# Value products of the wide attentions, stacked to full rows with 32-row bands in pairs

## The chip, the cores and the metric

One core of one Trainium2 chip. The time is device microseconds of one execution. Engines: PE is TensorE (PEld its weight loads), DVE VectorE, ACT ScalarE, POOL GpSimd, SP the queue that issues DMAs.

## The reference, cut to what matters

x has 128 sequences of 64 tokens with 128 features, the context `ctx_768` 128 sequences of 64 tokens with 96 features. Four layers follow each other, each an attention of x to the context and a feed-forward part, both added to x. The attentions that the change touches are L0 (8 heads of 128) and L2 and L3 (16 heads of 64):

```python
q = (layernorm(x) @ Wq) ; k = context @ Wk ; v = context @ Wv      # split into heads
attn = softmax(q k^T * scale)                                       # within a sequence, 64 x 64
x = x + (attn @ v).reshape(...) @ Wo + bo
```

## The kernel before, in words

`wide_attention` (L408) does one such attention. The product Wv Wo of each head is computed at its start ("fold": `fold_bank`, four heads a round, two rounds in L0, four in L2 and L3), so a value has 128 features per head: 96 context features times M. fp32 products that must be exact are made of three passes of a faster format (fp32r): high and low part of each operand, high*high, low*high, high*low (`product`, L285; its matmuls are L288, L290, L291). ScalarE keeps the high part of M (`keep_folded`, L690), VectorE the low one (`keep_rest`, L786). The context is loaded by SP in groups of 512 tokens, 96 rows (192 KB), and GpSimd splits it into high and low (`split_context`, L389 and L392), the next group's one while a group is worked on.

The 8192 tokens go in 16 groups of four tiles of 128 tokens. A group has Q steps of four heads, Q = 2 in L0 and 4 in L2 and L3 ("paired": two heads of 64 share 128 rows). That makes 32, 64 and 64 steps. In step m TensorE (`group` under `block.tensor`) does, in an order written out by hand: projections 0 and 1, three passes of 512 columns each; the transposes of the probabilities of step m - 2 (L577); projections 2 and 3; the four value products (`value`, three passes each, one PSUM bank per 128 tokens, each with 96 rows); the outputs of step m - 2 (L598, 64 matmuls in 64x64 tiles); the scores of step m (64 matmuls, in 64x64 tiles at L617, in L0 96x64 at L620). Values of four steps are held (`step % 4`). PSUM banks 4 to 7 rotate: P0, P1, T0, T1, P2, P3, V0 to V3 take them in turn, banks 0 and 1 are the scores', 2 and 3 the outputs'.

Besides, in each step: ScalarE copies projections (L708), transposed probabilities (L718) and values 0 and 2 (L713) out of PSUM and takes exponentials (L723); VectorE makes maxima and their subtraction (L810, L813), totals and inverses (L818, L821) and copies values 1 and 3 (L825), and once per group normalises and splits the next x (L254, L256); GpSimd multiplies probabilities by the inverses (L511). Every engine waits on semaphores that the others count up.

In L1 the narrow attention has scores in 32x64 tiles (L1030), which the change doesn't touch.

## Time and profile before

| | us |
|---|---|
| median of 3 runs (lowest, highest) | 3561.42 (3557.74, 3566.69) |
| the profiled execution | 3553.97 |
| its span, first to last instruction | 3552.1 |

The attentions of L0, L2 and L3 take about 353, 618 and 622 us of the span. A timeline row gives start, length, engine, line, operation, output and inputs, the part of the array (rows*columns of weights), the moving operand's shape and how many instructions are merged in it; a row of several runs from the first's start to the last's end. Matmuls overlap, so the distance of starts is what one costs.

### The profile page before, as it was taken

How to read it: one execution, taken by the hardware profiler on the slowest of the kernel's cores; microseconds unless marked ns; L12 is line 12 of the kernel's file. 1: busy time of each engine (PE TensorE's matmuls, PEld its weight loads, DVE VectorE, ACT ScalarE, POOL GpSimd, SP SyncE). 2: the span in 40 equal slices, each digit the busy share in tenths (PEclk: the TensorE clock that was granted, in tenths of full speed). 3: DMA queues.
4: the chain of work that ended last, by engine and by line, in shares of the span. 5: the costliest groups of instructions: out<-in, count | busy, mean ns of one | idle time of the engine just before them, and what ended most of it. 6: DMA issues, size and time to landing. Idle time of an engine off the chain costs nothing. (4 is left out here: it accounts for less than half of the span.)

```text
span 3552.1 us, 99744 instructions
## 1 busy us (share of the span) xinstructions
PE 3412.4 (96%) x43493; PEld 2808.9 (79%) x43493; DVE 2473.8 (70%) x4946; ACT 2033.0 (57%) x3467; POOL 1244.1 (35%) x923
## 2 busy tenths in 40 slices
PE   7999899999999899999999989999999998999999
PEld 6888788887888555788888878878888886777777
DVE  8977555555667799666666667766666666777776
ACT  4445555554666688455555545555555555566564
POOL 1322133334554233222222223322222224555555
PEclk9999999999999999999999999999999999999999
DMA  3000000001000000000000000010000000000000
GB/s 110 11 11 11 1 1 1 1 1 38 15 15 8 1 1 1 23 9 7 7 9 7 5 22 1 1 47 9 7 7 9 7 5 1 7 7 13 7 7 13
DMA packets 15488, 41.03 MB, mean 12 GB/s; under 512 B 2959, under 2 KB 4687, under 8 KB 14158
## 3 DMA queue, kind: packets, MB, share of 16 engines
q1 hardware_dynamic: 15054, 34.64, 3.2%
q8 instruction: 345, 5.65, 0.7%
q14 instruction: 89, 0.73, 0.1%
HBM read 30.44 MB, written 4.19 MB: 10 GB/s over the span
## 5 line engine op out<-in xcount | busy, mean ns | idle before, releaser
L708 ACT ACTIVATE projL<-bank 128x512 f32<-128x512 f32 (+1 forms) x640 | 371.3, 601 | 646.0 <-PE bank L291 630.4
L511 POOL TENSOR_TENSOR probL<-probL,invL 128x1024 f32<-128x1024 f32 x160 | 304.5, 1903 | 1196.5 <-DVE invL L821 1196.5
L1704 POOL TENSOR_TENSOR h_loM<-hM,h_hiM 126x512 fp32r<-126x512 f32 x224 | 290.3, 1296 | 254.7 <-ACT h_hiM L1830 252.0
L598 PEld LDWEIGHTS bank<-valuesL,probTL 64*64 64x64 f32 x10240 | 277.7, 133 | 60.9 <-issue 55.0
L810 DVE TENSOR_REDUCE neg_maxL<-bank 128x16 f32<-128x1024 f32 x160 | 195.9, 1224 | 183.7 <-PE bank L617 152.9
L598 PE MATMUL bank<-valuesL,probTL 64*64 64x128 f32 x10240 | 316.4, 272 | 4.4 <-ACT probTL L718 4.4
L1403 PEld LDWEIGHTS bank<-w2T,hM 128*128 128x128 f32 x2304 | 276.8, 192 | 39.3 <-ACT hM L1458 24.1
L1403 PE MATMUL bank<-w2T,hM 128*128 128x128 f32 x2304 | 283.4, 276 | 16.2 <-ACT hM L1458 16.2
L1458 ACT ACTIVATE hM<-bank,ahead_scales 128x512 f32<-128x512 f32 x288 | 183.8, 684 | 189.3 <-PE bank L291 189.0
L825 DVE COPY valuesL<-bank 128x512 f32<-128x512 f32 x320 | 213.1, 679 | 107.2 <-PE bank L291 101.3
L818 DVE TENSOR_REDUCE totalL<-probL 128x16 f32<-128x1024 f32 x160 | 194.8, 1217 | 122.4 <-ACT probL L723 122.1
L1381 POOL TENSOR_TENSOR accM<-accM,partM 128x512 f32<-128x512 f32 x128 | 165.0, 1289 | 295.5 <-DVE partM L1488 295.5
L1942 DVE TENSOR_TENSOR tM<-bank,siluM 126x512 f32<-126x512 f32 x224 | 154.2, 689 | 115.2 <-PE bank L291 64.6
L713 ACT ACTIVATE valuesL<-bank 128x512 f32<-128x512 f32 x320 | 195.4, 611 | 54.9 <-PE bank L291 54.2
L1830 ACT ACTIVATE h_hiM<-hM 126x512 fp32r<-126x512 f32 x224 | 140.6, 628 | 132.5 <-DVE hM L1966 131.3
L718 ACT ACTIVATE probTL<-bank 128x512 f32<-128x512 f32 x320 | 188.4, 591 | 24.9 <-PE bank L577 24.8
L813 DVE TENSOR_TENSOR probL<-bank,neg_maxL 128x1024 f32<-128x1024 f32 x160 | 195.9, 1225 | 5.5
L1824 ACT ACTIVATE siluM<-bank 126x512 f32<-126x512 f32 x224 | 132.0, 589 | 97.4 <-PE bank L291 95.7
L1488 DVE TENSOR_TENSOR partM<-bank,gatesM 128x512 f32<-128x512 f32 x128 | 88.4, 691 | 128.3 <-PE bank L1403 127.1
L723 ACT ACTIVATE probL<-probL 128x1024 f32<-128x1024 f32 x160 | 169.4, 1059 | 2.9 <-DVE probL L813 2.8
L577 PEld LDWEIGHTS bank<-ident,probL 128*128 128x128 f32 x1280 | 149.5, 141 | 24.0 <-POOL probL L511 1.8
L577 PE MATMUL bank<-ident,probL 128*128 128x128 f32 x1280 | 166.6, 273 | 0.5 <-POOL probL L511 0.3
(309 smaller groups left out, 9050.0 us busy)
## 6 DMA issues: line engine op xcount, KB each, us to landing
ct0L<-in_ctxP SPq DMA_DIRECT2D x24, 192.0 KB, 2.5
ct1L<-in_ctxP SPq DMA_DIRECT2D x24, 192.0 KB, 2.5
x<-in_x SPq DMA_DIRECT2D x4, 1024.0 KB, 10.9
out<-x SPq DMA_DIRECT2D x8, 512.0 KB, 2.6
nct<-in_ctxP SPq DMA_DIRECT2D x16, 192.0 KB, 2.4
ahead_second<-in_L0w SPq DMA_DIRECT2D x2, 1152.0 KB, 18.1
ahead_second<-in_L3gate SPq DMA_DIRECT2D x1, 882.0 KB
ahead_second<-in_L3up SPq DMA_DIRECT2D x1, 882.0 KB
```

The source lines that it names most:

```text
L511: nc.gpsimd.tensor_tensor(segments(prob[:, slot, :]), segments(prob[:, slot, :]), per_segment(inv[:, slot, :]), ALU.mult).then_inc(prob_re ...
L577: last = nc.tensor.transpose(rot.bank(step, f"T{half}")[:, u * P:(u + 1) * P], prob[:, prob_slot, cols], c.ident[:, :])
L598: last = nc.tensor.matmul(o_bank[b * SEQ:(b + 1) * SEQ, t, u * D:(u + 1) * D], probT[t * SEQ:(t + 1) * SEQ, 2 * s + u, b * SEQ:(b + 1) * SEQ],
L708: nc.scalar.activation(proj[:, u, :], rot.bank(step, f"P{u}")[0:rows, :], ACT.Copy, scale=scale if paired and u % 2 == 0 else 1.0).then_in ...
L713: nc.scalar.activation(values[:, step % 4, u, :, :].rearrange("p h d -> p (h d)"), rot.bank(step, f"V{u}")[:, :], ACT.Copy).then_inc(Veven ...
L718: nc.scalar.activation(probT[:, 4 * half:4 * half + 4, :].rearrange("p s q -> p (s q)"), rot.bank(step, f"T{half}")[:, :], ACT.Copy).then_ ...
L810: nc.vector.tensor_reduce(neg_max[:, prob_slot, :], segments(s_bank.rearrange("p h c -> p (h c)")), axis=AX.X, op=ALU.max, negate=True).th ...
L813: nc.vector.tensor_tensor(segments(prob[:, prob_slot, :]), segments(s_bank.rearrange("p h c -> p (h c)")), per_segment(neg_max[:, prob_slo ...
L818: nc.vector.tensor_reduce(total[:, prob_slot, :], segments(prob[:, prob_slot, :]), axis=AX.X, op=ALU.add).then_inc(total_ready, 1)
L825: nc.vector.tensor_copy(values[:, step % 4, u, :, :].rearrange("p h d -> p (h d)"), rot.bank(step, f"V{u}")[:, :]).then_inc(Vodd_kept, 1)
L1403: last = nc.tensor.matmul(y_bank[ex % NY][:, t * D:(t + 1) * D], h[:, (n + j) % NH, t * P:(t + 1) * P], W2[:, 2 * ex + j, :], start=(t == ...
L1704: nc.gpsimd.tensor_tensor(h_lo[:, a % SLOTS, :], h[:, a % 3, :], h_hi[:, a % SLOTS, :].bitcast(F32), ALU.subtract).then_inc(lo_ready, 1)
```

## The change

The value product of 128 tokens is no longer three passes over 96 rows. Three operands of 128 rows are stacked instead. With H and L the high and low parts and a, b, c the three 32-row bands of the 96 context features:

- T1 holds Ha Hb Hc La, M1 the matching Ha Hb Hc Ha: one full pass;
- T2 holds Ha Hb Lb Lc, M2 the matching La Lb Hb Hc: one full pass;
- T3 holds Hc alone, the band u of it (rows 32u to 32u + 31) that of token tile u, M3 has Lc four times: one pass of 32 rows for each tile, done for tiles 0 and 1 together after the second tile, and for 2 and 3 after the fourth.

SP loads the context three times stacked (A and B with 128 rows, 256 KB each, C 64 KB), GpSimd rounds and subtracts in place (`stack_context`); in paired layers it also keeps `ct_lo` for the projections. The outputs of step m - 2 move ahead of value product 3. Values are held for three steps. The folded rounds are kept by three copies and five differences each, on VectorE; in L2 and L3 rounds 2 and 3 are done in steps 1 and 2, and TensorE waits for each round by itself. The fourth fold bank moves from bank 7 to banks 0 to 3. VectorE splits the next x before it copies value 3.

```diff
@@ wide_attention @@
-        M_hi, M_lo = (sb(f"M{n}{tag}", [K, heads, D], F32R) for n in ("_hi", "_lo"))
+        M1, M2, M3 = (sb(f"M{n}{tag}", [P, heads, D], F32R) for n in (1, 2, 3))
...
-        values = sb(f"values{tag}", [P, 4, 4, 4, D])
+        values = sb(f"values{tag}", [P, 3, 4, 4, D])
...
-        fold_bank = (c.bank[1], c.bank[2], c.bank[3], c.bank[7]) if paired else (c.bank[1], c.bank[3])
+        fold_bank = c.bank[0:4] if paired else (c.bank[1], c.bank[3])
+        parts = 6 if paired else 5
@@ block.sync @@
-                first_contexts(sp, c, "ctxP", ct, ct_in)
+                def load_context(j):
+                    for dst, name in zip(raw[j % 2], ("ctxA", "ctxB", "ctxC")):
+                        cols = dst.shape[1]
+                        sp.dma_start(dst[:, :], dram[name][:, j * cols:(j + 1) * cols]).then_inc(ct_in[j % 2], 16)
+
+                load_context(0)
+                load_context(1)
...
-                later_contexts(sp, c, "ctxP", ct, ct_in, S_done, Q, 0)
+                for j in range(2, NG):
+                    sp.wait_ge(S_done, (j - 1) * Q)
+                    load_context(j)
@@ block.gpsimd @@
+                def stack_context(j, slot):
+                    A, B, C = raw[slot]
+                    pool.wait_ge(ct_in[slot], 48 * (j // 2 + 1))
+
+                    def high_part(part, high):
+                        nc.gpsimd.tensor_tensor(high[:, :], part[:, :], c.one[:, :].to_broadcast([P, part.shape[1]]), ALU.mult)\
+                            .then_inc(ct_split, 1)
+
+                    high_part(A, T1[slot])
+                    if paired:
+                        pool.wait_ge(ct_split, parts * j + 1)
+                        nc.gpsimd.tensor_tensor(ct_lo[slot][:, :], A[0:K, :], T1[slot][0:K, :].bitcast(F32), ALU.subtract)\
+                            .then_inc(ct_split, 1)
+                    high_part(B, T2[slot])
+                    high_part(C, T3[slot])
+                    for n, (part, high, rows) in enumerate(((A, T1[slot], slice(96, P)), (B, T2[slot], slice(64, P)))):
+                        pool.wait_ge(ct_split, parts * (j + 1) - 2 + n)
+                        nc.gpsimd.tensor_tensor(high[rows, :], part[rows, :], high[rows, :].bitcast(F32), ALU.subtract)\
+                            .then_inc(ct_split, 1)
+                    pool.wait_ge(ct_split, parts * (j + 1))
@@ block.tensor @@
-                    pe.wait_ge(lo_kept, 2 * rounds)
+                    pe.wait_ge(lo_kept, rounds)
...
-                    weights = tuple(M[:, 4 * k:4 * k + 4, :].rearrange("p h d -> p (h d)") for M in (M_hi, M_lo))
-                    product(nc, rot.bank(step, f"V{u}")[:, :], (ct_hi[slot][:, tok], ct_lo[slot][:, tok]), weights)\
-                        .then_inc(V_done, 1)
+                    for n, (tokens, weights) in enumerate(((T1, M1), (T2, M2))):
+                        nc.tensor.matmul(rot.bank(step, f"V{u}")[:, :], tokens[slot][:, tok],
+                                         weights[:, heads_of, :].rearrange("p h d -> p (h d)"), start=(n == 0), stop=False,
+                                         skip_group_check=True)
+
+                def values_rest(slot, k, step, pair):
+                    for u in (2 * pair, 2 * pair + 1):
+                        band = slice(32 * u, 32 * u + 32)
+                        nc.tensor.matmul(rot.bank(step, f"V{u}")[:, :], T3[slot][band, :],
+                                         M3[band, 4 * k:4 * k + 4, :].rearrange("p h d -> p (h d)"), start=False, stop=True,
+                                         skip_group_check=True).then_inc(V_done, 1)
...
-                            pe.wait_ge(ct_split, 2 * i + 2)
...
+                        if k == 0 and paired:
+                            pe.wait_ge(ct_split, parts * i + 2)
...
-                        if m == 0 and paired:
-                            pe.wait_ge(lo_kept, 6)
+                        if k == 0:
+                            pe.wait_ge(ct_split, parts * (i + 1))
+                        if i == 0:
+                            pe.wait_ge(stack_kept, k + 1)
                         value(m, slot, k, 0, step)
                         pe.wait_ge(T_kept, 2 * m + 2)
                         value(m, slot, k, 1, step)
+                        values_rest(slot, k, step, 0)
                         pe.wait_ge(P_kept, 4 * m + 7)
                         value(m, slot, k, 2, step)
                         if older:
                             wait_for_output(n, *back)
+                            if paired and i == 0 and k == 2:
+                                pe.wait_ge(stack_kept, 4)
+                            output(n, back[0], back[1], n % 3)
                         wait_for_scores(m, i, k)
                         value(m, slot, k, 3, step)
-                        if older:
-                            output(n, back[0], back[1], bstep % 4)
+                        values_rest(slot, k, step, 1)
+                        if paired and i == 0 and k == 0:
+                            pe.wait_ge(stack_kept, 2)
                         scores(m, i, slot, k)
@@ block.vector @@
+                def stack_copies(r):
+                    dve.wait_ge(hi_kept, r + 3 if paired else 2 * r + 2)
+                    for M, to, rows in ((M1, slice(96, P), slice(0, 32)), (M2, slice(64, 96), slice(32, 64)),
+                                        (M2, slice(96, P), slice(64, 96))):
+                        nc.vector.tensor_copy(flat(M, to, r), fold_bank[r][rows, :])
+
+                def stack_differences(r):
+                    nc.vector.tensor_tensor(flat(M2, slice(0, 64), r), fold_bank[r][0:64, :],
+                                            flat(M1, slice(0, 64), r).bitcast(F32), ALU.subtract)
+                    for u in range(4):
+                        last = nc.vector.tensor_tensor(flat(M3, slice(32 * u, 32 * u + 32), r), fold_bank[r][64:96, :],
+                                                       flat(M1, slice(64, 96), r).bitcast(F32), ALU.subtract)
+                    last.then_inc(stack_kept, 1)
...
-                keep_rest(0)
-                keep_rest(1)
-                if paired:
-                    keep_rest(2)
-                    keep_rest(3)
+                    keep_rest(0)
+                    keep_rest(1)
                     for scale_step in scale_steps:
                         scale_step()
                 else:
+                    keep_low_queries(0)
+                    keep_low_queries(1)
+                    stack_copies(0)
                     split_transposed(nc, dve, c, 0, 0, xT_ready, xT_split)
+                    stack_differences(0)
+                    keep_rest(1)
...
+                        if paired and i == 0 and k in (1, 2):
+                            keep_rest(k + 1)
...
-                        keep_value(m, 3, step)
                         if k == Q - 1:
                             split_transposed(nc, dve, c, i + 1, 1 - slot, xT_ready, xT_split)
+                        keep_value(m, 3, step)
```

## Rows read from the trace of the kernel before

**Rows 1.** Page, part 1: each engine's busy time and share.
```profile
PE 3412.4 (96%) x43493; PEld 2808.9 (79%) x43493; DVE 2473.8 (70%) x4946; ACT 2033.0 (57%) x3467; POOL 1244.1 (35%) x923
```

**Rows 2.** Table by stage: window; length; engines' busy us; PEclk; DMA share; GB/s.
```profile
27.00:380.00 353.00, 342.93 (x5103) 280.81 (x5102) 290.13 (x611) 181.05 (x310) 93.34 (x59) 1.00 0.04 10
39.00:100.00 61.00, 54.86 (x781) 44.46 (x784) 57.28 (x157) 29.72 (x51) 15.05 (x9) 0.97 0.04 12
1444.00:2062.00 618.00, 615.49 (x10252) 520.72 (x10251) 413.06 (x694) 344.20 (x597) 153.45 (x93) 1.00 0.03 7
2328.00:2950.00 622.00, 618.83 (x10323) 524.01 (x10322) 414.12 (x698) 343.36 (x595) 153.45 (x92) 1.00 0.03 8
```

**Rows 3.** Waits of TensorE, attention of L2: us in total, times, longest.
```profile
PE bank L288 <- ACT probTL L718: 1.1, 1, 1.1
```

**Rows 4.** Timeline, TensorE, one step of L3: start us, us, engine, line, instruction.
```profile
2599.80 1.11 PE L617 MATMUL bank<-projL 64*64 64x64 f32 x64
...
2604.60 0.39 PE L288 MATMUL bank<-M_hiL,ct_hi1L 96*128 96x512 f32 x1
...
2607.11 0.39 PE L291 MATMUL bank<-M_loL,ct_hi1L 96*128 96x512 f32 x1
2607.43 1.98 PE L598 MATMUL bank<-valuesL,probTL 64*64 64x128 f32 x64
2609.23 1.11 PE L617 MATMUL bank<-projL 64*64 64x64 f32 x64
```

**Rows 5.** Timeline close up, scores to projection, L3.
```profile
2600.45 0.46 PE L617 MATMUL bank<-projL 64*64 64x64 f32 x18
...
2600.84 0.50 PE L288 MATMUL bank<-xT_hi,wq_hiL 128*128 128x512 f32 x1
...
2601.17 0.40 PE L290 MATMUL bank<-xT_hi,wq_loL 128*128 128x512 f32 x1
```

**Rows 6.** Timeline close up, values to outputs, L3.
```profile
2607.43 0.34 PE L598 MATMUL bank<-valuesL,probTL 64*64 64x128 f32 x4
```

**Rows 7.** Timeline, TensorE, end of a step of L0.
```profile
207.83 1.98 PE L598 MATMUL bank<-valuesL,probTL 64*64 64x128 f32 x64
209.74 2.13 PE L620 MATMUL bank<-ct0L,projL 96*64 96x64 f32 x64
211.80 0.47 PE L288 MATMUL bank<-xT_hi,A_hiL 128*96 128x512 f32 x1
212.11 0.39 PE L290 MATMUL bank<-xT_hi,A_loL 128*96 128x512 f32 x1
```

**Rows 8.** Timeline, end of L3's fold, at half clock.
```profile
2324.85 0.84 PE L541 MATMUL bank<-ahead_first 64*96 64x128 f32 x3
...
2325.62 0.79 PE L288 MATMUL bank<-xT_hi,wq_hiL 128*128 128x512 f32 x1
...
2326.21 0.63 PE L290 MATMUL bank<-xT_hi,wq_loL 128*128 128x512 f32 x1
```

**Rows 9.** Groups by line: line, engine, op, shapes, count; busy us, mean ns; idle before.
```profile
L598 PE MATMUL bank<-valuesL,probTL 64*64 64x128 f32 x10240 | 316.4, 272 | 4.4 <-ACT probTL L718 4.4
L511 POOL TENSOR_TENSOR probL<-probL,invL 128x1024 f32<-128x1024 f32 x160 | 304.5, 1903 | 1196.5 <-DVE invL L821 1196.5
...
L1030 PE MATMUL bank<-kT,qm 32*64 32x64 f32 x4096 | 74.9, 220 | 0.0
...
L392 POOL TENSOR_TENSOR ct_lo1L<-ct1L,ct_hi1L 96x512 fp32r<-96x512 f32 x24 | 31.7, 1323 | 1.9
...
L389 POOL TENSOR_TENSOR ct_hi1L<-ct1L,one 96x512 fp32r<-96x512 f32 x24 | 25.4, 1060 | 0.0
```

**Rows 10.** Lines L541 and L786: ns min/median/max, first and last start.
```profile
L541 PE MATMUL bank<-ahead_first x64: 269/417/418, 1437.5 to 2325.3; 64*96 64x128 f32 x64
...
L786 DVE TENSOR_TENSOR M_loL<-bank,M_hiL x10: 674/686/687, 17.7 to 2326.4; 96x512 fp32r<-96x512 f32 x10
```

**Rows 11.** Timeline, VectorE's first value copy in L3, its idle time.
```profile
2332.31 0.69 DVE L825 COPY valuesL<-bank 128x512 f32<-128x512 f32 x1 [3.03 <-PE bank L291]
```

More of the change, by code:

```diff
@@ L430, in wide_attention @@
         bo = sb(f"bo{tag}", [P, D])
-        ct = [sb(f"ct{s}{tag}", [K, GT]) for s in range(2)]
-        ct_hi, ct_lo = ([sb(f"ct{n}{s}{tag}", [K, GT], F32R) for s in range(2)] for n in ("_hi", "_lo"))
+        raw = [[sb(f"ct{n}{s}{tag}", [P, cols]) for n, cols in (("A", GT), ("B", GT), ("C", P))] for s in range(2)]
+        T1, T2 = ([sb(f"T{n}{s}{tag}", [P, GT], F32R) for s in range(2)] for n in (1, 2))
+        T3 = [sb(f"T3{s}{tag}", [P, P], F32R) for s in range(2)]
+        ct_lo = [sb(f"ct_lo{s}{tag}", [K, GT], F32R) for s in range(2)] if paired else None
         proj = sb(f"proj{tag}", [rows, 4, GT])
-        values = sb(f"values{tag}", [P, 4, 4, 4, D])
+        values = sb(f"values{tag}", [P, 3, 4, 4, D])
         prob = sb(f"prob{tag}", [P, 2, 4 * 4 * SEQ])
@@ L505, in _ @@
                     pool.wait_ge(one_set, 1)
-                for j in range(2):
-                    split_context(nc, pool, c, ct, ct_hi, ct_lo, j, j, 0, ct_in, ct_split)
+                def stack_context(j, slot):
[16 more added lines that the diff above has]
+                    pool.wait_ge(ct_split, parts * (j + 1))
+                stack_context(0, 0)
+                stack_context(1, 1)
                 def multiply(n, slot):
@@ L518, in group @@
                         if k == 1 and turn is not None:
[L519 removed]
+                            stack_context(i + 1, 1 - slot)
                 group(0, 0)
@@ L552, in projection @@
                     x_parts = c.xT_hi[slot][:, :], c.xT_lo[slot][:, :]
-                    ct_parts = ct_hi[slot][:, :], ct_lo[slot][:, :]
+                    ct_parts = (T1[slot][0:K, :], ct_lo[slot][:, :]) if paired else None
                     out = rot.bank(step, f"P{u}")[0:rows, :]
@@ L619, in scores @@
                                     else:
-                                        last = nc.tensor.matmul(out, proj[:, 2 * h + p, tok], ct[slot][:, ctx],
+                                        last = nc.tensor.matmul(out, proj[:, 2 * h + p, tok], raw[slot][0][0:K, ctx],
                                                                 start=True, stop=True)
@@ L675, in _ @@
                     wait_for_output(n, n // Q, n % Q)
-                    output(n, n // Q, n % Q, n % 4)
+                    output(n, n // Q, n % Q, n % 3)
                 keep_warm(nc, c, rot.bank(NS + 1, "T0"), 15)
@@ L712, in keep_value @@
                     act.wait_ge(V_done, 4 * m + u + 1)
-                    nc.scalar.activation(values[:, step % 4, u, :, :].rearrange("p h d -> p (h d)"),
+                    nc.scalar.activation(values[:, m % 3, u, :, :].rearrange("p h d -> p (h d)"),
                                          rot.bank(step, f"V{u}")[:, :], ACT.Copy).then_inc(Veven_kept, 1)
@@ L775, in _, with keep_low_queries @@
                 scale_steps = scales.steps(dve)
-                def keep_rest(r):
-                    hs = slice(r * 4, (r + 1) * 4)
-                    if not paired:
-                        dve.wait_ge(hi_kept, 2 * r + 1)
-                        nc.vector.scalar_tensor_tensor(out=A_lo[:, hs, :].rearrange("p h k -> p (h k)"),
-                                                       in0=c.bank[2 * r][:, 0:4 * K], scalar=scale,
-                                                       in1=A_hi[:, hs, :].bitcast(F32).rearrange("p h k -> p (h k)"),
-                                                       op0=ALU.mult, op1=ALU.subtract).then_inc(lo_kept, 1)
-                    dve.wait_ge(hi_kept, r + 3 if paired else 2 * r + 2)
-                    nc.vector.tensor_tensor(M_lo[:, hs, :].rearrange("p h d -> p (h d)"), fold_bank[r][0:K, :],
-                                            M_hi[:, hs, :].bitcast(F32).rearrange("p h d -> p (h d)"), ALU.subtract)\
-                        .then_inc(lo_kept, 1)
+                def keep_low_queries(r):
+                    hs = slice(r * 4, (r + 1) * 4)
+                    dve.wait_ge(hi_kept, 2 * r + 1)
+                    nc.vector.scalar_tensor_tensor(out=A_lo[:, hs, :].rearrange("p h k -> p (h k)"),
+                                                   in0=c.bank[2 * r][:, 0:4 * K], scalar=scale,
+                                                   in1=A_hi[:, hs, :].bitcast(F32).rearrange("p h k -> p (h k)"),
+                                                   op0=ALU.mult, op1=ALU.subtract).then_inc(lo_kept, 1)
@@ new lines, in flat @@
+                def flat(M, rows, r):
+                    return M[rows, r * 4:(r + 1) * 4, :].rearrange("p h d -> p (h d)")
+                def stack_copies(r):
[3 more added lines that the diff above has]
+                        nc.vector.tensor_copy(flat(M, to, r), fold_bank[r][rows, :])
@@ L790, in _ @@
+                def keep_rest(r):
+                    stack_copies(r)
+                    stack_differences(r)
                 if paired:
@@ L824, in keep_value @@
                     dve.wait_ge(V_done, 4 * m + u + 1)
-                    nc.vector.tensor_copy(values[:, step % 4, u, :, :].rearrange("p h d -> p (h d)"),
+                    nc.vector.tensor_copy(values[:, m % 3, u, :, :].rearrange("p h d -> p (h d)"),
                                           rot.bank(step, f"V{u}")[:, :]).then_inc(Vodd_kept, 1)
```

9 lines of the change are left out of this document (6 added, 3 removed).

## The prediction

> **What bounds the kernel now.** I read the page's busy shares first: TensorE is busy 96% of the span, GpSimd 35% [rows 1]. The table by stage then shows that this is no average over different limits: in the attentions of L2 and L3 TensorE works 615.49 of 618 us and 618.83 of 622 us, in L0's 342.93 of 353, at full clock (column PEclk), DMA at 3 to 4% [rows 2]. Only L0's beginning differs: from 39 to 100 us VectorE is busy 57.28 of 61. The list of waits confirms it: over all of L2's attention TensorE's longest wait is 1.1 us, once [rows 3]. So in the wide attentions a microsecond on TensorE's queue is a microsecond of the kernel, and the change must be priced there, instruction by instruction.
>
> The close timeline gives the prices. One step of a paired layer (L2, L3) takes 2609.23 - 2599.80 = 9.43 us. Within it the twelve value products run without a gap, from 2604.60 to 2607.11 eleven starts later: **0.228 us each** [rows 4], though only 96 of 128 rows are used. Around the two blocks that use a part of the array the pace breaks. *Into* 64x64 tiles: 0.32 us from the last value product to the first output matmul, 0.09 more than a pace [rows 4], and the first four outputs span 0.34 us [rows 6], where one takes 0.272 on average [rows 9] and the four start some 0.02 apart: another 0.05, a weight load of 64 columns that nothing hides. I call it **0.14**. *Out of* tiles: 64 scores span 1.11 us [rows 4] and the last 18 of a step 0.46 [rows 5], so their starts are (1.11 - 0.46)/46 = 0.014 apart and one lasts 0.22; they end at 2600.91, so the last began at 2600.69, and the next full-array matmul stands at 2600.84: 0.15 later, of which about 0.06 is the pace of a group of four scores, 0.09 the break. That matmul takes 0.50 where its successor takes 0.40, and the successor comes after 0.33 instead of 0.228: 0.10 for an exposed load of 128 columns [rows 5]. Together **0.20**. L0 agrees: output to scores 1.91 instead of 1.80 (its scores use 96x64 tiles, another shape, so a break), scores to projection 0.31 to the next start [rows 7].
>
> **The unknown: does a 32-row band of full width break the pace as well?** No instruction of before has that shape. Nearest is the fold of the weights, 64 rows and 96 columns: three of its matmuls span 0.84 us and one takes 0.417 [rows 8, 10], so they start 0.21 apart and the last at 2325.27; the next full one stands at 2325.62, 0.35 later instead of 0.21, and that one's successor 0.59 later where 0.43 is the pace [rows 8]. That is half clock, but the same two parts, 0.14 and 0.16, so a tile of rows alone pays too. I take 0.20 for every entry of a band or a full product after another shape. The other bound is nothing. The Trainium skill, TensorEngine Tiling (Array Packing), Key Properties, says that changing the tiling mode drains the engine while changing the tile alone doesn't; rows 5, 6 and 8 agree. The same skill, TensorE: Matmul & The Clock Gate, Measured speedup vs the span model, prices packed tiles at one matmul and about 4 ns per further tile, with no drain; by that alone this change would gain (rival B).
>
> Do two bands run side by side? The first four outputs go to four tiles and end within 0.34 us [rows 6] though one takes 0.272, so starts are at most some 7 ns apart once the load's 0.05 is off; L1's scores, 32x64 tiles, last 0.220 each and 4096 of them are busy only 74.9 us, 0.018 apiece [rows 9]. So a pair costs 0.228 + 0.007 = 0.235; the other bound is 0.456.
>
> **The change, part by part, per paired step.** (1) Twelve passes become eight: -4 x 0.228 = -0.912. (2) Two pairs of bands: +0.470. (3) Breaks. Before: values to outputs 0.14, (outputs to scores same shape, none), scores to projection 0.20. After: values 0,1 to bands 0.20; bands to value 2 0.20; to outputs 0.14; outputs to value 3 0.20; to bands 0.20; bands to scores 0.14; to projection 0.20. That is +4 x 0.20 + 0.14 = +0.94. Sum **+0.50 us**, 128 steps: +64. In L0 bands to scores replaces outputs to scores, so (3) is +0.80 and the sum +0.36, 32 steps: +11.5. Off go the two first steps of each layer, which have no outputs (6 x 0.34 = 2) and L0's five or six steps between 39 and 100 us, where VectorE sets the pace (2). **Steady state: +71 us.**
>
> (4) Folding. Each round's one difference, 0.686 us [rows 10], becomes three copies and five differences. They have fewer partitions but the same 512 elements in each, so I take the same 0.686: 5.5 us a round, +4.8. L0 has two rounds, +9.6 us on VectorE just ahead of the stretch it bounds; the new order lets the first transposes go before the two differences they waited for, so I count 8. L2 and L3 have four. Two fall before the first scores, where VectorE idles 3.03 us before its first value copy [rows 11] and has time in the first step; about 2 us remains. Rounds 2 and 3 stand in steps 1 and 2, ahead of totals and value copies that TensorE's next step waits for; the round-3 difference is also awaited by the first output. VectorE has 1 - 413.06/618 = 33% of a step free [rows 2], 3.2 us of 5.5: 2.3 late each, about 5. So 7 a layer. **Start-up: +22**; bounds 5 (hidden but for L0) and 35 (all of 9.6 + 2 x 12).
>
> (5) Costed at nothing. GpSimd: per group it now has three high parts, up to three differences, about 1.1 + 1.3 + 1.1 + 0.3 + 1.3 + 1.3 = 6.4 us instead of 2.4. It runs behind a multiply of 1.90 [rows 9] once in four steps (two in L0); with both, 8.3 of 9.9 us are filled, and the multiply itself has most of a step before its transposes, so TensorE doesn't see it. If VectorE delays it beyond that, transposes wait. SP: three context DMAs for one, 576 KB for 192, a group ahead on queues 3 to 4% busy [rows 2]; nothing queued behind but the next group's. At L0's start six issues stand where two did, ahead of x's later parts, some 2 us on loads needed much later. Waits: outputs between tiles 2 and 3 wait for probabilities kept long before (TensorE waits for them once now, 1.1 us [rows 3]); V2 and V3 are now finished only at the scores, but their copies (0.69 each) have scores and two projections, 2.7 us, before the transposes need the banks. Three value slots suffice, since output n precedes the products that refill them.
>
> **Sum.** The profiled execution took 3553.97 us (span 3552.1), 7.4 below the median of the three runs, 3561.42. +71 + 22 = +93 gives 3647 against the one, 3654 against the other; I forecast **3652 us**.
>
> **Rivals.**
> A, the forecast: breaks as priced, 72%. Its own range 3620 to 3690.
> B, the other side: a full-width band needs no drain (the array's columns are not divided, and the next weights slip in under the running stream). Then (3) is only outputs to value 3 and one more into 64x64: +0.34 per paired step, +0.20 in L0; sums -0.10 and -0.24, together -21; with start-up at its low bound +5, 3561 - 16 = 3545 us. For it: 64x64 also divides columns, bands don't. Against: rows 8. It decides if an entry into or out of a band costs under about 0.1 us. 12%: by where start-up falls, faster in 8, same in 4.
> C, bands one after the other: 320 pairs x 0.221 = +71 more, 3723 us. For it: both load 128 columns. Against: rows 6 and 9. 8%.
> D, GpSimd becomes late: a group's 6.4 us push a multiply past its transposes, 1 us in each of 48 groups: 3700. Against: 1196.5 us of GpSimd waiting for inverses [rows 9]. 8%.
>
> **Numbers.** Low 3580, high 3715: that holds A and D, 80%, and leaves out B and C. About 0.3% (11 us) is what a measurement of this kernel can tell from no change. Faster 0.08 and same 0.04 (B), slower 0.88 (A, C, D).
>
> **What would show it.** Right: paired steps of 9.9 us instead of 9.43, a gap of 0.3 us from the last full product to the first band, band pairs starting 7 ns apart, the next full product about 0.75 us after the last one before the pair began; TensorE's busy share unchanged or lower; VectorE waited for in steps 1 to 2 of L2 and L3 only. Wrong: weight loads of T2 or T3 that begin under a running stream across a change of shape (B), bands 0.2 us apart (C), or TensorE waiting for the multiply at L511 (D).

## The result, and the profile after

The kernel after takes **3688.4 us** (median of 4 runs, 3687.08 to 3697.13), the kernel before, run beside it, 3564.06 (3557.74 to 3568.88): a ratio of **1.0359, 95% interval 1.034 to 1.0377**. The profiled spans are 3686.2 and 3552.1 us, so 134 us are to be explained. The forecast was slower, 3652; the sign and the cause were right, the size was short by about a third.

The page's first part, in the form of [rows 1]:

```profile
PE 3521.1 (96%) x43493; PEld 2728.2 (74%) x43493; DVE 2574.6 (70%) x5016; ACT 2052.0 (56%) x3467; POOL 1418.1 (38%) x1099
```

TensorE does as many matmuls as before (eight full passes and four bands for twelve) and is busy 109 us longer: a matmul's busy time holds the weight load that nothing covers (0.50 us for 0.40 in the rows below). The table by stage, in the columns of [rows 2]:

```profile
27.00:398.00 371.00, 357.99 (x5094) 264.96 (x5096) 306.98 (x653) 184.84 (x311) 136.59 (x101) 0.99 0.08 25
...
1474.00:2140.00 666.00, 658.55 (x10247) 485.37 (x10248) 444.21 (x708) 350.21 (x594) 210.37 (x150) 0.99 0.05 15
2413.00:3079.00 666.00, 658.59 (x10248) 485.25 (x10248) 443.96 (x707) 350.30 (x594) 210.12 (x150) 0.99 0.05 15
```

The same matmuls take 666 us in L2 and L3 where they took 618 and 622, in L0 371 for 353. These three windows hold 110 of the 134 us. Most of the rest lies just before those of L2 and L3, where the weights are folded. One step of L3, TensorE's timeline (the counterpart of [rows 4]; L660 scores, L604 full value products, L611 bands, L641 outputs):

```profile
2688.68 1.16 PE L660 MATMUL bank<-projL 64*64 64x64 f32 x64
...
2694.67 0.39 PE L604 MATMUL bank<-M2L,T20L 128*128 128x512 f32 x1
2694.99 0.50 PE L611 MATMUL bank<-M3L,T30L 32*128 32x512 f32 x2
2695.42 0.50 PE L604 MATMUL bank<-M1L,T10L 128*128 128x512 f32 x1
2695.75 0.40 PE L604 MATMUL bank<-M2L,T20L 128*128 128x512 f32 x1
2696.08 1.98 PE L641 MATMUL bank<-valuesL,probTL 64*64 64x128 f32 x64
2697.99 0.50 PE L604 MATMUL bank<-M1L,T10L 128*128 128x512 f32 x1
2698.32 0.40 PE L604 MATMUL bank<-M2L,T20L 128*128 128x512 f32 x1
2698.65 0.50 PE L611 MATMUL bank<-M3L,T30L 32*128 32x512 f32 x2
```

Each entry shows two marks. After a full pass the next shape starts 0.32 to 0.33 us later instead of 0.23. And the first full product or band of its block takes 0.50 where its successor, which finds its load covered, takes 0.40; after a full product's entry that successor also starts 0.33 later instead of 0.23. Two bands span 0.50, as long as one instruction: they run side by side. From the last full product before the pair to the next one after it, 2695.42 - 2694.67 = 0.75.

The usual distance from scores to scores, without the first steps and one long one of each attention: L2 and L3 10.21 us (before 9.56), L0 11.18 (10.76). That is 0.65 and 0.43 a step where +0.50 and +0.36 were forecast. Most of the difference is a wait that nobody had touched. The next step of L3, at value product 1:

```profile
2703.79 0.60 ACT L769 ACTIVATE probTL<-bank 128x512 f32<-128x512 f32 x1
...
2704.17 0.40 PE L604 MATMUL bank<-M2L,T21L 128*128 128x512 f32 x1
...
2704.43 0.19 PEld L604 LDWEIGHTS bank<-M1L,T11L 128*128 128x128 f32 x1 [0.31 <-ACT probTL L769]
2704.44 0.50 PE L604 MATMUL bank<-M1L,T11L 128*128 128x512 f32 x1
...
2704.77 0.40 PE L604 MATMUL bank<-M2L,T21L 128*128 128x512 f32 x1
```

Product 1 waits for ScalarE's copy of the second half of the probabilities (L769), which ends at 2704.39. The products got shorter, so product 1 comes a pass sooner, and the copy doesn't. Here the wait costs 0.04 and the load it uncovers 0.10. So it is in two of a group's four paired steps; in the third (k = 2, k being the number of a step in its group) the product starts 0.13 late, and in k = 3 it does not wait. TensorE's weight-load waits over the whole run (us in total, times, longest):

```profile
PEld bank L611 <- issue: 116.7, 320, 0.7
PEld bank L641 <- issue: 61.4, 154, 2.7
PEld bank L604 <- ACT probTL L769: 43.7, 108, 1.7
```

The 320 idle times before L611 are the entries into the bands.

**The start of L2 and L3** is most of the rest. L3 before its first scores:

```profile
2408.25 2.79 DVE L849 TENSOR_TENSOR M3L<-bank,M1L 32x512 fp32r<-32x512 f32 x4
...
2411.07 0.80 DVE L346 TENSOR_SCALAR var_eps<-stats 128x64 f32<-128x64 f32 x1
...
2411.91 0.26 ACT L330 ACTIVATE root<-var_eps 128x64 f32<-128x64 f32 x1 [7.36 <-DVE var_eps L346]
2412.07 1.06 ACT L759 ACTIVATE projL<-bank 128x512 f32<-128x512 f32 x2
2412.80 0.77 PE L288 MATMUL bank<-xT_hi,wq_hiL 128*128 128x512 f32 x1 [6.01 <-ACT projL L759]
```

The folding of rounds 0 and 1 stands ahead of `var_eps` on VectorE; ScalarE's square root waits for that, 7.36 us, and the projection copies stand behind the root on ScalarE; TensorE waits 6.01 us for them. The windows of six microseconds show it, TensorE 0.20 us busy and its granted clock 0.50; its passes stay at the half-clock length of 0.63 us until 2415.5, in the kernel before until 2330.0:

```profile
2407.00:2413.00 6.00, 0.20 (x1) 0.23 (x2) 5.54 (x9) 1.09 (x3) 5.69 (x7) 0.50 1.00 220
2413.00:2419.00 6.00, 6.00 (x32) 4.01 (x36) 3.35 (x7) 2.06 (x5) 1.79 (x2) 0.74 0.16 44
```

The kernel before in the same place:

```profile
2326.00:2332.00 6.00, 6.00 (x18) 4.65 (x18) 2.43 (x8) 3.32 (x7) 0.00 (x0) 0.64 0.96 217
```

Then steps 1 and 2 start as forecast: waits of TensorE over L2's attention, against the single one of 1.1 us in [rows 3]:

```profile
PE bank L288 <- ACT projL L759: 5.7, 1, 5.7
PE bank L641 <- DVE M3L L849: 2.3, 1, 2.3
PE bank L288 <- DVE valuesL L894: 1.7, 1, 1.7
...
PE bank L620 <- POOL probL L546: 0.4, 1, 0.4
```

**Half the clock, after a wait.** Once in each attention of L2 and L3 the scores stand 13.1 us apart instead of the usual 10.2; in the kernel before the same stretch takes 10.8. In both kernels ScalarE is late there and value product 1 waits for it, before 1.08 us, now 1.29:

```profile
2930.25 0.50 PE L604 MATMUL bank<-M1L,T10L 128*128 128x512 f32 x1 [1.29 <-ACT probTL L769]
...
2932.40 3.17 PE L641 MATMUL bank<-valuesL,probTL 64*64 64x128 f32 x64
```

After it the 64 output matmuls take 3.17 us instead of 1.98. The windows of 3 us (columns of [rows 2]; the first is the changed kernel, the second the kernel before, at the same outputs) give the cause, a granted clock of 0.52, which is the lower of TensorE's two levels (1.2 GHz) for almost the whole window, where before has the full 2.4 GHz:

```profile
2932.00:2935.00 3.00, 3.00 (x54) 2.60 (x56) 2.03 (x4) 0.04 (x1) 1.34 (x1) 0.52 0.02 5
```

```profile
2809.00:2812.00 3.00, 3.00 (x119) 2.65 (x121) 1.92 (x4) 0.50 (x1) 1.90 (x1) 1.00 0.02 5
```

Such a stretch costs about 1.6 us: in root_early, below, the same scores of L2 stand 11.53 us apart without one, 13.14 here with one. The trace of the changed kernel has five that the kernel before lacks: one late in each of the three attentions, and one in step 1 of L2 and of L3, where the wait of 2.3 us comes first.

**The account of the 134 us**, from the starts of scores in both traces: L0's start 7; before the first scores of L2 and L3 8.3 + 6.7; their first steps 7.5 each (from the scores of step 1 to the next 17.03 for 9.53); steps after that +11.5 in L0 and +41 each in L2 and L3; 3 to 4 elsewhere. The half-clock stretches, 8 us together, are in these terms.

### The profile page after: what moved, and what is told of

Read it like the earlier page. It is cut to its first block and busy times, and to the rows that moved or that the text cites. A ratio compares the mean times of both kernels' runs of the same rounds, so it can differ in the third digit from the quotient of the medians.

```text
span 3686.2 us, 100170 instructions
## 1 busy us (share of the span) xinstructions
PE 3521.1 (96%) x43493; PEld 2728.2 (74%) x43493; DVE 2574.6 (70%) x5016; ACT 2052.0 (56%) x3467; POOL 1418.1 (38%) x1099
## 5 line engine op out<-in xcount | busy, mean ns | idle before, releaser
L641 PEld LDWEIGHTS bank<-valuesL,probTL 64*64 64x64 f32 x10240 | 283.3, 135 | 67.2 <-issue 61.4
L641 PE MATMUL bank<-valuesL,probTL 64*64 64x128 f32 x10240 | 322.3, 276 | 9.1 <-DVE M3L L849 4.6
L769 ACT ACTIVATE probTL<-bank 128x512 f32<-128x512 f32 x320 | 188.2, 590 | 18.3 <-PE bank L620 18.3
## 6 DMA issues: line engine op xcount, KB each, us to landing
x<-in_x SPq DMA_DIRECT2D x4, 1024.0 KB, 10.8
```

The costliest lines, as they stand in the source:

```text
L641: last = nc.tensor.matmul(o_bank[b * SEQ:(b + 1) * SEQ, t, u * D:(u + 1) * D], probT[t * SEQ:(t + 1) * SEQ, 2 * s + u, b * SEQ:(b + 1) * SEQ],
L769: nc.scalar.activation(probT[:, 4 * half:4 * half + 4, :].rearrange("p s q -> p (s q)"), rot.bank(step, f"T{half}")[:, :], ACT.Copy).then_ ...
```

## Experiments

"Steps" are usual distances from scores to scores in L2 and L3, counted as above; k is that of the scores at the end. "Step 0" and "step 1" at the start of a layer are counted from their own scores to the next.

**outputs_last: two breaks fewer.** The outputs go back behind product 3, next to the scores.

```diff
-                            output(n, back[0], back[1], n % 3)
                         wait_for_scores(m, i, k)
                         value(m, slot, k, 3, step)
                         values_rest(slot, k, step, 1)
+                            output(n, back[0], back[1], n % 3)
```

> The changed kernel with the outputs of step m - 2 put back behind value product 3 and its bands; all else as changed. Theory (every change of the array's shape costs 0.20 us when it leads to 128 columns of weights and 0.14 when it leads to 64): of the seven such changes in a paired step two go, 0.34 us, in L0 0.20 us; 128 x 0.34 + 32 x 0.20 = 50 us less than the changed kernel, about 3638 us. Rival (the steps grew because TensorE waits for ScalarE's copies, and shapes cost nothing): within 10 us of the changed kernel's 3688.

Measured: 3629.78 us (3627.03 to 3643.66), 1.0199 of before (1.0156 to 1.0241). Steps 9.82 for 10.21: -0.39, L0 10.99 for 11.18. Moving 64 matmuls by one product gave back 59 us. By rival B, with the outputs' move gone and no price on the bands' entries, the kernel would be below the time of before even with the start as measured; it isn't.

**before_moved: the same two breaks, alone, on the kernel before.**

```diff
                         if older:
                             wait_for_output(n, *back)
+                            output(n, back[0], back[1], bstep % 4)
                         wait_for_scores(m, i, k)
                         value(m, slot, k, 3, step)
-                        if older:
-                            output(n, back[0], back[1], bstep % 4)
```

> The kernel before with nothing changed but the place of the outputs: ahead of value product 3 instead of behind it. Theory: two more changes of shape in a paired step (0.34 us), one more of 0.20 in L0, 50 us more than the kernel before, about 3614 us. Rival (shapes cost nothing): the same time as before, 3564.

Measured: 3635.37 us (3633.31 to 3644.57), 1.0222 (1.0185 to 1.0259). The steps that show only the breaks (k = 1, 2) grow from 9.43 and 9.48 to 9.83 and 9.84: +0.37 to 0.40. The rest is a wait of its own, in k = 0 (+1.17), from the list of TensorE's waits:

```profile
PE bank L288 <- DVE xT_lo L256: 28.9, 35, 2.2
```

Value 3 now comes after the outputs, VectorE splits the next tokens behind its copy, and the next group's first projection waits. In the change the split goes ahead of that copy; this run shows the wait that this order spares.

**four_bands: one block of four bands.** The outputs behind, and all four bands after product 3.

```diff
                         value(m, slot, k, 1, step)
-                        values_rest(slot, k, step, 0)
...
                         value(m, slot, k, 3, step)
+                        values_rest(slot, k, step, 0)
                         values_rest(slot, k, step, 1)
+                            output(n, back[0], back[1], n % 3)
```

> The changed kernel with all four bands in one block behind value product 3, and the outputs behind them. Theory of the shape changes: a paired step has 3 instead of 7 (0.54 instead of 1.28 us) and one run of four bands (0.25) instead of two of two (0.47), L0 the same with 0.68 instead of 1.28; 128 x 0.96 + 32 x 0.82 = 149 us less than the changed kernel, about 3540 us and so faster than the kernel before by 25 us. New waits for ScalarE (the values now need their banks sooner) could give back up to 0.25 us a step, 3580. If four bands don't run side by side: 0.46 us a step more, 3610. Rival (waits only): no less than 3670.

Measured: **3565.36 us** (3561.51 to 3577.19, 10 runs), 1.0026 (1.0009 to 1.0043). Steps 9.39, another -0.43, and now below before's 9.56. Its timeline at the block:

```profile
2537.37 0.40 PE L604 MATMUL bank<-M2L,T21L 128*128 128x512 f32 x1
2537.70 0.50 PE L611 MATMUL bank<-M3L,T31L 32*128 32x512 f32 x4
2538.13 1.10 PE L641 MATMUL bank<-valuesL,probTL 64*64 64x128 f32 x32
```

Four bands span what two do: 0.50. From its first band to the next shape a block takes 0.43 us with two bands or with four, so the second block of the change was pure loss. The 123 us won are 26 fewer than expected. Steps k = 0 to 2 fell by 0.96 on average, as priced, but k = 3 only from 10.41 to 10.02, and L0's steps by 0.57 for 0.82. Part of what holds k = 3 back is seen below, under four_tuned.

**no_bands: the whole price of the bands.** The kernel leaves the third operand's term out of the values.

```diff
-                        values_rest(slot, k, step, 0)
...
-                        values_rest(slot, k, step, 1)
```

> The changed kernel without the bands: the term high part times low part of context features 64 to 95 is left out of the values, everything else stays. It prices the two pairs. Theory: the first pair costs 0.235 and two entries of 0.20, the second 0.235 and one entry of 0.20, 1.07 us a step in all 160 steps, 171 us less than the changed kernel, about 3517 us. Rival (bands stream between full products without a break): 160 x 0.47 = 75 us less, 3613 us.

Measured: 3539.63 us (3531.89 to 3543.91), 0.9933 (0.9908 to 0.9957). Steps 9.25, -0.96 of the 1.07 expected. The two blocks, with the breaks around them, cost nearly an entire microsecond of each step.

**exp_later: the unforeseen wait.** On ScalarE the copy of the probabilities' second half goes ahead of the exponentials.

```diff
-                        if k or started(i, 1):
-                            exponentials(m - 1, (step - 1) % 2)
                         if older:
                             keep_probs(m - 2, 1, step)
+                        if k or started(i, 1):
+                            exponentials(m - 1, (step - 1) % 2)
```

> The changed kernel with one exchange on ScalarE: the copy of the second half of the transposed probabilities goes before the exponentials instead of behind them. In three of four paired steps value product 1 now stands 0.13 us behind that copy and its weight load is then exposed, 0.11 more. Theory: that is the part of the steps' growth which the shape changes don't explain; it goes in 96 steps of L2 and L3 and 16 of L0, 25 us less than the changed kernel, about 3663 us. Rival (the exponentials, now later, hold up totals, multiply and transposes): the same or more than 3688.

Measured: 3662.23 us (3659.99 to 3667.22), 1.0269 (1.0236 to 1.0301). Steps 10.08 for 10.21, and L0 11.10 for 11.18; 26 us in all. So of the 0.15 a step beyond the forecast the wait was 0.13. Some 17 of the 26 us are that; most of the rest is the single long stretch, which falls to 10.9 us in L2 and L3, with no half clock after its wait, and its like in L0.

**root_early: the chain before the first scores.** In L2 and L3 `scale_steps[0]()` runs ahead of the folding.

```diff
+                    scale_steps[0]()
                     keep_rest(0)
                     keep_rest(1)
-                    for scale_step in scale_steps:
-                        scale_step()
+                    scale_steps[1]()
```

> The changed kernel with one exchange on VectorE at the start of L2 and L3: the sum of variance and epsilon, for which ScalarE's square root waits, goes before the folding of rounds 0 and 1 instead of behind it. Theory: the square root stands in ScalarE's queue ahead of the first projection copies, so TensorE waited 6.0 us for them in each of the two layers; 12 us less than the changed kernel, about 3676 us. Rival (the start is bound by VectorE's folding itself): within 3 us of 3688.

Measured: 3670.68 us (3668.43 to 3677.51), 1.0295 (1.0267 to 1.0323), 18 us less. ScalarE's idle time before the first projection copy of L3 falls to 0.84 us:

```profile
2394.22 0.24 ACT L330 ACTIVATE root<-var_eps 128x64 f32<-128x64 f32 x1
2395.30 0.60 ACT L759 ACTIVATE projL<-bank 128x512 f32<-128x512 f32 x1 [0.84 <-PE bank L291]
```

The first steps give a little back (9.61 and 18.03 in L2 for 7.88 and 17.01): the folding itself is not shorter. By the starts of scores the edit is worth 12.5 us, as expected; some 3 more come from two half-clock stretches, late in L0 and L2, which this execution happens not to have and which the edit does not touch.

**four_waits_gone: all of it, and a miss.** four_bands with the early root, the probabilities' second half earlier, and the exponentials not before but behind the copies of projections 2 and 3.

```diff
-                        if k or started(i, 1):
-                            exponentials(m - 1, (step - 1) % 2)
                         if older:
                             keep_probs(m - 2, 1, step)
...
                         keep_projection(m, 3, step)
+                        if k or started(i, 1):
+                            exponentials(m - 1, (step - 1) % 2)
                         keep_value(m, 0, step)
```

> All four bands in one block, outputs behind it, the sum of variance and epsilon early, and the exponentials behind all of a step's projection copies. In the run with four bands in a block TensorE lost 0.24 us a step to the copy of probabilities and 0.6 us in every fourth step to the copy of projection 3. Theory: 12 us at the starts, 0.16 x 96 + 0.6 x 32 = 34 us in the steps less than that run's 3565, about 3519 us, 1.2% below the kernel before. Rival (exponentials so late hold up the next transposes): 3550 or more.

Measured: **3635.06 us** (3624.27 to 3640.63), 1.019 (1.0163 to 1.0216). Steps k = 1 and 2 are the shortest of all, 8.98, but k = 0 takes 10.1 and k = 3 11.3 or 12.9. TensorE's waits:

```profile
PE bank L288 <- DVE xT_lo L256: 48.6, 46, 3.4
PE bank L288 <- DVE valuesL L894: 39.4, 34, 5.6
PE bank L620 <- POOL probL L546: 21.3, 34, 0.7
```

In its timeline VectorE, with the totals later, comes to the normalising of the next tokens (L220) just when GpSimd stacks the next context:

```profile
2563.75 1.27 POOL L531 TENSOR_TENSOR ct_lo1L<-ctA1L,T11L 96x512 fp32r<-96x512 f32 x1
...
2564.98 1.04 POOL L525 TENSOR_TENSOR T21L<-ctB1L,one 128x512 fp32r<-128x512 f32 x1
2565.16 4.04 DVE L220 TENSOR_SCALAR xh<-x,stats,rstd 128x128 f32<-128x128 f32 x4
```

The same four instructions in the kernel before, with nothing on GpSimd beside them:

```profile
2574.58 1.11 DVE L220 TENSOR_SCALAR xh<-x,stats,rstd 128x128 f32<-128x128 f32 x4
```

Three microseconds late, the totals, the value copies and the split follow in VectorE's queue, and TensorE waits for each. That the two engines together make it slow was seen in the traces, not tried by itself. The 12.9 is the clock: in 14 steps k = 3 it falls after TensorE's waits of 0.78 and 0.63 us. In the steps of 11.3 us it stays full after waits of the same length. One of the 14:

```profile
1652.00:1655.50 3.50, 3.47 (x14) 3.10 (x15) 1.33 (x2) 1.54 (x4) 0.00 (x0) 0.52 0.00 0
```

At 1.6 us each these are some 22 us of this run.

**four_start_short** adds to that the folded copies on ScalarE, from the high part in SBUF, and the differences of rounds 2 and 3 at the ends of steps 0 and 1.

```diff
+                        if paired and m == 0:
+                            copy_folded(1)
                         keep_value(m, 0, step)
                         keep_value(m, 2, step)
+                        if paired and m < 2:
+                            copy_folded(m + 2)
```

> The kernel with the waits gone, and in L2 and L3 the three folded copies of a round made by ScalarE from the high part in SBUF instead of by VectorE from PSUM, rounds 2 and 3 at the ends of steps 0 and 1. VectorE's folding falls from 5.5 to 3.4 us a round. Theory: most of the 7.5 us that steps 1 and 2 lost in each of L2 and L3 goes, 4 to 6 us a layer, 3509 us. Rival (ScalarE's twelve copies of 0.6 us take the place of what they relieve): no less than 3519.

Measured: 3628.82 us (3622.85 to 3641.18), 1.018 (1.0154 to 1.0206). In L2 step 1 falls from 16.5 to 11.5 us, in both layers steps 0 and 1 together by some 5 us, and little else changes: the start was not what had gone wrong.

**four_tuned, four_root_copies, four_tuned_copies: which of the edits carry over.** four_bands with the root early and exp_later's order; with the root early and the copies on ScalarE; with all three.

```diff
# four_tuned: exp_later + root_early on four_bands
# four_root_copies: root_early + copy_folded on four_bands
# four_tuned_copies: exp_later + root_early + copy_folded on four_bands
```

> The version with all four bands in one block (3565 us), with the VectorE part of the square root ahead of the folding, and with ScalarE's copy of the second half of the probabilities ahead of its exponentials (both as in the runs that did one of them alone, on the changed kernel). Unlike the version that missed, the exponentials stay ahead of the copies of projections 2 and 3. If the two gains carry over, as the single runs give them (18 and 26 us on the changed kernel; here the wait for the second half stands in front of value product 1 in three of four steps at about 0.2 us, so 20 of the 26), it takes 3565 - 18 - 20 = 3527 us, range 3520 to 3545, and the paired steps k = 0 to 2 take 9.05 to 9.1 us instead of 9.18. Rival: the two copies in front of the exponentials delay the totals and the copy of value product 1 enough that VectorE meets GpSimd's stacking of the context again, as in the version that missed: then k = 3 takes over 11 us and k = 0 10 us, and the time is 3600 to 3640 us.

> The version with all four bands in one block, with VectorE's part of the square root ahead of the folding, and with the three folded copies of each round on ScalarE (from the high part in SBUF) and the differences of rounds 2 and 3 at the ends of steps 0 and 1; the exponentials stay where the change has them. If the start of L2 and L3 is what the copies cost (each of step 1's rounds 2.0 us of copies less on VectorE, some 5 us a layer as in the earlier version with a short start) and the root gives 9 us in all, it takes 3565 - 9 - 10 = 3546 us, range 3535 to 3555, with step 1 of L2 and L3 at 10 to 11.5 us and steps k = 3 at 10.0. Rival: ScalarE, now with six more copies in the first steps, is late for the projections instead, and the start stays as long: 3556 us, step 0 or 1 as long as before in sum.

> All of it: four bands in one block, the square root early, ScalarE's copy of the second half of the probabilities ahead of its exponentials, the folded copies on ScalarE. If the gains add up: 3527 - 10 = 3517 us, range 3510 to 3540, below the kernel before by 1.2%. Rival: steps k = 3 and k = 0 as long as in the version that missed: 3600 to 3630 us.

Measured: 3560.23 (3554.06 to 3578.56), 3558.97 (3551.16 to 3574.74) and 3563.15 us (3557.19 to 3582.91), 12 runs each; ratios 1.0004 (0.9986 to 1.0023), 0.9996 (0.9977 to 1.0015) and 1.0007 (0.9988 to 1.0026). None reached its number, and none is told apart from the kernel before. But four_tuned differs from four_waits_gone in the exponentials' place alone, 3560 for 3635: it is that delay, and not the early root or the early copy, that costs the 75 us. VectorE meeting GpSimd is not by itself the reason, since it happens in the better versions too. The next tokens' normalising in four_bands, usual and in the one group of L3 where it misses the stacking, and in four_tuned:

```profile
2515.12 2.57 DVE L220 TENSOR_SCALAR xh<-x,stats,rstd 128x128 f32<-128x128 f32 x4
...
2818.39 1.11 DVE L220 TENSOR_SCALAR xh<-x,stats,rstd 128x128 f32<-128x128 f32 x4
```

```profile
2594.56 3.09 DVE L220 TENSOR_SCALAR xh<-x,stats,rstd 128x128 f32<-128x128 f32 x4
```

In the group that misses it, step k = 3 takes 9.67 us instead of 10.02, in four_tuned 9.76 instead of 10.33: the meeting seems to cost some 0.35 and 0.55 us a group there (the one group differs in that the long stretch comes just before), and nothing in the changed kernel (1.77 us, k = 3 at 10.41 with it and without). What makes four_waits_gone so much worse, the 4.04 us or all of VectorE's later work, was not separated. The gain of exp_later does not add: in four_tuned steps k = 0 to 2 take 9.17 to 9.18 as in four_bands, and k = 3 10.33 for 10.02. TensorE and ScalarE in one of its steps:

```profile
2586.95 1.09 ACT L759 ACTIVATE projL<-bank 128x512 f32<-128x512 f32 x2
2587.09 0.39 PE L604 MATMUL bank<-M1L,T10L 128*128 128x512 f32 x1
2587.32 0.40 PE L604 MATMUL bank<-M2L,T20L 128*128 128x512 f32 x1
2587.61 0.50 PE L604 MATMUL bank<-M1L,T10L 128*128 128x512 f32 x1
2587.95 0.40 PE L604 MATMUL bank<-M2L,T20L 128*128 128x512 f32 x1
```

Product 1 is at pace now (2587.09), but product 2 stands 0.06 us for the copy of projection 2, which the exponentials pushed back, and its load of 0.10 lies open instead: the wait moved by one product. Without that 0.16, by these numbers, the step would be at the 9.0 of four_waits_gone. In the changed kernel the first bands stand between products 1 and 2 and had covered it. In four_root_copies the rival came true: step 1 takes 14.3 and 15.6 us, and step 0 10.8 and 12.9 for the 7.9 of four_bands, so what comes sooner before the first scores is lost behind them.

**four_P3_first: the last step of a group.** On four_root_copies, ScalarE copies projection 3 ahead of the transposed tokens, and TensorE waits for these only at the scores.

```diff
                         if k == Q - 1:
...
+                            keep_projection(m, 3, step)
                             keep_transposed(nc, act, c, xt_bank, i + 1, 1 - slot, xt_done, xT_ready, affine)
-                        keep_projection(m, 3, step)
+                        else:
+                            keep_projection(m, 3, step)
@@ block.tensor @@
-                    if k == Q - 1:
-                        pe.wait_ge(xT_ready, i + 2)
...
+                        if k == Q - 1:
+                            pe.wait_ge(xT_ready, i + 2)
                         scores(m, i, slot, k)
```

> The version with the four bands in one block, the early root and the folded copies on ScalarE (3559 us), and in the last step of each group ScalarE copies projection 3 ahead of the transposed tokens (xT), with TensorE's wait for xT moved from value product 3 to the scores. In that step value product 3 now starts 530 ns after the product before it and the next one 335 ns after it, where the pace is 232: 0.40 us, the wait for ScalarE's copy of projection 3, which stands behind xT (in L0 0.25 us). If that wait is gone and none takes its place: 32 x 0.40 + 15 x 0.25 = 17 us, so 3559 - 17 = 3542 us, range 3536 to 3550, steps k = 3 at 9.6 us instead of 10.02 (0.60 of what is left over 9.18 being the transposes of the tokens, with their entry), about 0.5% below the kernel before. Rival: VectorE gets the tokens later, its split and the copy of value product 3 behind it come later, and the first steps of the next group wait for them: k = 0 then grows by what k = 3 loses, and the time stays at 3559.

Measured: **3548.46 us** (3540.5 to 3559.39, 12 runs) beside 3564.79 for the kernel before: ratio **0.9959 (0.9942 to 0.9976)**, 0.4% below the kernel before, small but clear of no change, and within the range expected. Steps k = 3 take 9.63 for 10.02, the others stay at 9.18 to 9.19. In L0 the rival came true: k = 1 falls by 0.27 and k = 0 rises by 0.27. The same exchange on ScalarE was not tried on the kernel before, so how much of the 0.4% the stacking has earned is open.

## Why the prediction was right, and where it fell short

**The bound** (TensorE's queue) held: what the steps and starts lost or won above came out in the time.

**Steps (1) and (2)** held. The two bands of a pair start 3 to 4 ns apart (0.007 us was taken), and four span 0.50 us as well. Rival C is out.

**Step (3)**, the one that decided the sign, held. An entry into a band costs 0.094 of drain (0.326 us against 0.232) and 0.107 of open load, in all 320 entries: 0.20, as taken from the full-clock rows [rows 5], and the fold's half-clock rows [rows 8] were right that a tile of rows alone pays. The Trainium skill, TensorEngine Tiling (Array Packing), Key Properties, says that changing the mode drains the engine; the runs agree, also for a band that divides only the rows. The Trainium skill, TensorE: Matmul & The Clock Gate, Measured speedup vs the span model, prices packed tiles without an entry; inside a block that holds (3 ns for the second band), but the entry comes on top. Rival B is out by these entries and by four_bands, where one block fewer gave back 0.43 us a step. before_moved confirms the breaks around the outputs, which B priced too: 0.37 to 0.40 us a step where 0.34 was taken.

**Step (5), "costed at nothing", is the step that failed in steady state.** It priced the waits that the change adds and moves, not the one that stays: `T_kept` ahead of value product 1. With two passes for three, that product comes 0.23 us sooner and meets ScalarE's copy in three of four paired steps. It is 0.13 of the 0.15 by which the step exceeded its forecast, some 17 us, and exp_later got them back. What no term of the sum held is the clock: one half-clock stretch late in each attention, 5 us. GpSimd, in the same step, did cost nothing (one wait of 0.4 us in L2): rival D is out for the changed kernel. In its faster versions GpSimd's longer work does cost, by stretching VectorE's normalising.

**Step (4)** was right for L0 (8 forecast, 7 measured), for a round (5.5 us) and nearly for steps 1 and 2 (5 forecast, 7.5 measured, of which 4.0 are the waits of 2.3 and 1.7 us for VectorE and about 1.6 a half-clock stretch behind the first), and **wrong in "about 2 us remains"** before the first scores. VectorE's idle 3.03 us [rows 11] were not the cover that counted: the folding stands in front of `var_eps`, and through the root in ScalarE's queue it held the projections: 8.3 and 6.7 us. root_early showed it: 12.5 us in its trace, 18 in the medians. Of a step that grows, the engines *behind* it in other queues had to be followed, not only its own engine's idle time.

Sum: +71 +22 forecast; +93.5 and +37 in the trace. The last 3 to 4 us of the 134 lie mostly between the end of L0 and the fold of L2, in code that the change leaves alone, and were not explained. Not tried, and so open, is whether a later stacking on GpSimd would keep four_waits_gone's steps of 8.98 without its collision.

## What to carry to other kernels

Count the changes of shape on TensorE before counting passes: here an entry costs 0.14 to 0.20 us, nearly a pass of 512 columns (0.23), so here bands paid only in one block, placed next to another tiled block (steps k = 0 to 2 at 9.18 us for 9.43 to 9.48 before). When work on the bounding engine gets shorter, go through the waits that stay and ask which now comes too early; when work on another engine gets longer, follow what stands behind it through every queue. And try combinations: gains of 18 and 26 us on the changed kernel gave 5 on its better version, hardly more than the spread, and the place of the exponentials on ScalarE alone makes 75 us between four_tuned and four_waits_gone.

## What the runs showed that was not expected

- A wait that is hardly one still costs 0.10 us on TensorE: product 1 started 0.04 late, but took 0.50 and delayed the next start to 0.33, since its weights were loaded only after the wait.
- VectorE's SBUF-to-SBUF work stretched beside GpSimd's tensor operations: four L220 took 1.77, 2.57, 3.09 and 4.04 us for 1.11 in four kernels, and L346 0.80 for 0.18 at the start of L3 (changed kernel against before). VectorE's copies out of PSUM beside the same work took no more than their 0.69.
- A wait of TensorE near a microsecond can cost more than itself: after 1.29 us the granted clock was at its lower level for the next matmuls (0.52 in the window), after 1.08 us in the kernel before it was not. It is not the length alone: after the same 0.78 and 0.63 us in four_waits_gone it fell in 14 groups and stayed full in others.
